# Two cross attentions: every transposed probability block evicted by VectorE, with new written-out orders

## The chip, the cores and the metric

The kernel runs on one core of one Trainium2 chip. The metric is the device time of one execution in microseconds (us), from the start to the end of the program on that core; the median of a few executions is given. Shorter is better. Engines are TensorE (PE in the rows, its weight loads PEld), VectorE (DVE), ScalarE (ACT), GpSimd (POOL) and SyncE (SP, which only issues DMAs here).

## The reference, cut to what matters

A decoder of two layers on x of 16 batches x 256 positions x 512 features, all float32. In order: causal self attention with rotary embedding, causal cross attention, an expert layer, a normalised linear attention, a cross attention without mask, an fp8 linear layer. The change concerns the two cross attentions:

```python
Q = heads(layernorm(x) @ Wq.T + bq); K = heads(ctx @ Wk.T + bk); V = heads(ctx @ Wv.T + bv)   # 16 heads of 32
scores = Q @ K.T / sqrt(32)            # 256 x 256 per head; the first cross attention adds a causal mask
attn = softmax(scores)                 # over the keys
x = x + merge_heads(attn @ V) @ Wo.T + bo   # the first cross attention has no biases
```

## The kernel before, in words

The program is a sequence of phases, one per layer part; each phase is one call that loads its weights, runs over the 16 batches and ends with a barrier over all engines. `attention_phase` builds the self attention ("self") and the two cross attentions ("cross0", causal, and "cross1"). A batch is 256 query positions (two blocks of 128), 16 heads. In a cross attention four heads share one 128-row group g, so there are four groups.

Inside a phase nothing is scheduled at run time. Each engine walks through a written-out order, `ORDERS[phase][engine]`, once per round, a round being one batch in the steady state; a "+" after a step means that it is done for the next batch, a "-" for the batch before. `over_batches` runs a first round that holds only "+" steps, 16 full rounds (the middle ones in a hardware loop) and a last one with only "-" steps. Engines meet only by semaphores. The steps, by their name in the orders:

- X0, X1, C0, C1: TensorE transposes the normalised x or the context into a projection bank (L485); ScalarE writes the high part (L661), VectorE the low part (L735), because projections are made as three products of high and low parts (L73 to L75).
- Q0 to Q3: query and key projection of a group, 24 matmuls; ScalarE evicts Q (L670, L672), VectorE K (L757, L759). V00, V01: values, evicted by VectorE (L750). O0, O1: output projection, added to the residual by VectorE (L768).
- S0 to S3: scores of the four heads of a group into four banks, one per head (L562, with mask L569). A group needs all four banks, so it waits until the exponentials of the group before are done.
- max h (VectorE, L809 or L811), exp h (ScalarE, L678, with the row sums), inv h (VectorE reciprocal, L816), norm h (GpSimd, L431): the softmax of head h.
- T h: TensorE transposes the probabilities of head h into the single bank TP (L590): three 128x128 blocks in cross0, four in cross1. take h: TP is copied to `probT` in SBUF, by ScalarE (L685) or VectorE (L821). T of head h+1 waits for the take of head h (`wait_taken`, in `prob_transposes`).
- PV g: probabilities times values of four heads into the single bank Z (L608); it waits for the takes of its heads and for Z to be free. z g: ScalarE evicts the high part of Z (L692, L694), VectorE the low part (L832, L834).

The projection banks are two and used in turn by the X, C, Q, V and O steps in TensorE's order; class `Uses` counts these uses. A wait for bank use u is a wait on semaphore `a_free` for a count, and since batches run in a loop the count is (batch times uses per batch) plus a constant; `after` makes such a wait. Before the change, ScalarE's order holds the takes of the odd heads and VectorE's those of the even ones in both cross attentions. PV then waits on two semaphores, `pt_act` and `pt_dve`.

Of the kernel before, what the change touches and what calls it, by code (L numbers as in the profile page):

```python
# [30 lines left out]
T = S // P  # L31
# [92 lines left out]
class Uses:  # L124
# [13 lines left out]

    def at(self, key, n):
        i = self.place(key)  # L140
        return (n + (1 - self.keys[i][1])) * self.n + self.before + i
# [5 lines left out]
    def adds(self, key, n):  # L147
# [4 lines left out]
        while True:  # L152
# [3 lines left out]
            if r > self.n_batch or batch_of(r, self.keys[i][1], self.n_batch) is not None:  # L156
# [29 lines left out]
                "Q2 T13- S1 T14- PV2- T15- Q3 T0 PV3- X0+ T1 S2 T2 X1+ V00 T3 V01 T4 S3 T5 O0- C0+ T6 PV0 C1+ T7 O1- T8 Q0+ T9 "  # L186
                "Q1+ T10 S0+ T11 PV1 T12"),
        "ACT": (
                "exp3 Q2 take13- z2- take15- exp4 exp5 exp6 Q3 exp7 X0+ take1 X1+ exp8 exp9 exp10 exp11 take3 z3- take5 exp12 "
                "C0+ exp13 C1+ take7 z0 Q0+ take9 exp14 exp15 Q1+ take11 exp0+ z1 exp1+ exp2+"),  # L190
        "DVE": (
# [3 lines left out]
        "POOL": (  # L195
                "norm10- norm11- norm12- norm13- norm14- norm15- norm0 norm1 rstd+ norm2 norm3 norm4 norm5 norm6 norm7 norm8 "
                "norm9"),
# [3 lines left out]
                "T11- S0 T12- Q2 T13- PV2- T14- Q3 T15- S1 T0 X0+ PV3- T1 V01 T2 V00 T3 S2 C0+ T4 O0- C1+ T5 PV0 X1+ T6 O1- T7 "  # L201
                "S3 T8 Q0+ T9 PV1 T10 Q1+"),
        "ACT": (
                "exp0 exp1 exp2 take13- Q2 z2- exp3 Q3 take15- X0+ z3- take1 exp4 exp5 exp6 exp7 take3 C0+ exp8 exp9 C1+ take5 "
                "exp10 exp11 X1+ z0 take7 exp12 Q0+ take9 exp13 exp14 exp15 Q1+ take11 z1"),
        "DVE": (
# [10 lines left out]
def attention_phase(nc, name, n_batch, x_in, x_out, consts, wq, wk, wv, wo,  # L217
# [42 lines left out]
    with Phase(nc, name) as ph:  # L260
# [195 lines left out]
        def _(pe):  # L456
            pe.wait_ge(const_in, 16 * N_CONST)

            def bank_for(key, n):

                u = uses.at(key, n)
                if not isinstance(u, int) or u > 1:
                    pe.wait_ge(a_free, u - 1)
                return A[uses.bank(key)]
# [1323 lines left out]
```

## Time and profile before

| what | value |
|---|---|
| median of 3 runs | 4003.99 us (4002.36 to 4004.89) |
| the profiled execution | 4007.67 us, its span 4005.9 us |
| mean granted TensorE clock | 0.921 of full speed |
| busy share PE, PEld, DVE, ACT, POOL | 86%, 60%, 49%, 32%, 35% |
| cross0, from its first barrier to its last | about 1251.6 to 1933.6 us of the span |
| cross1, likewise | about 3140.5 to 3853.5 us |
| self attention; experts and linear attention between; fp8 layer | before 1251; 1934 to 3140; after 3854 us |

The span runs from the first to the last instruction; the 1.8 us between it and the execution's own time lie around it. Busy shares are means over all phases. Matmuls overlap one another, so PE busy for 100% of a stretch says that no gap was seen, not that the array is at its peak; whether it waits is read from the idle time before an instruction and from the distance between starts. A duration given for a VectorE or ScalarE instruction includes its start and its end, which overlap with the neighbours, so that back-to-back instructions start closer together than they last.

### The profile page before, as it was taken

The page shows a single profiled execution, that of the slowest core. Times are in us where ns is not written, and L with a number is a line of the kernel's source. Part 1 is how long each engine was busy: PE and PEld are TensorE (multiplying, and loading weights), DVE is VectorE, ACT ScalarE, POOL GpSimd, SP SyncE. Part 2 cuts the span into 40 slices and gives each one's busy share as a digit, 9 for nine tenths or more (in the row PEclk, how much of TensorE's full clock was granted, in tenths as well). Part 3 has the DMA queues.
Part 4 walks back from the last instruction along what each step waited for, and adds up shares of the span by engine and source line. Part 5 has one row for each costly group of instructions (what it writes and reads, how often), then busy time and mean ns, then how long its engine had stood idle before and what let it go on. Part 6 is the DMA issues. An engine that isn't in the chain of part 4 may idle for free. (4 is left out here: it accounts for less than half of the span.)

```text
span 4005.9 us, 71048 instructions
## 1 busy us (share of the span) xinstructions
PE 3444.4 (86%) x23116; PEld 2412.7 (60%) x23116; DVE 1974.0 (49%) x4934; ACT 1263.5 (32%) x4320; POOL 1408.4 (35%) x2092
## 2 busy tenths in 40 slices
PE   4999999999997999999667666655999699999955
PEld 3776776776764888888352111113777578888831
DVE  5555554554553665666420000002666466666667
ACT  2222232232222555555100000001111266666621
POOL 2554554554551443343100000000222155555537
PEclk9999999999997999999857877877999799999976
DMA  5000000000002111110459999994121211111113
GB/s 126 22 16 16 31 16 24 24 16 31 16 11 86 36 60 54 50 63 32 164 173 425 427 427 427 427 427 184 69 70 63 83 37 58 42 63 42 53 66 131
DMA packets 158786, 459.15 MB, mean 115 GB/s; under 512 B 47392, under 2 KB 51872, under 8 KB 138208
## 3 DMA queue, kind: packets, MB, share of 16 engines
q1 hardware_dynamic: 150272, 445.72, 29.3%
q10 hardware_dynamic: 8448, 12.59, 0.9%
q8 instruction: 36, 0.59, 0.1%
q14 instruction: 30, 0.25, 0.0%
HBM read 402.17 MB, written 56.10 MB: 114 GB/s over the span
## 5 line engine op out<-in xcount | busy, mean ns | idle before, releaser
L431 POOL TENSOR_TENSOR cross_prob<-cross_prob,cross_rsum 128x256 f32<-128x256 f32 (+1 forms) x1024 | 547.1, 562 | 725.8 <-DVE cross_rsum L816 721.6
L678 ACT ACTIVATE cross_prob<-cross_S,cross_neg_max 128x256 f32<-128x256 f32 (+1 forms) x1024 | 444.1, 457 | 53.6 <-DVE cross_neg_max L811 46.2
L431 POOL TENSOR_TENSOR self_prob<-self_prob,self_rsum 128x128 f32<-128x128 f32 (+1 forms) x512 | 246.3, 506 | 193.7 <-DVE self_rsum L816 189.4
L590 PE MATMUL cross_T<-cross_ident,cross_prob 128*128 128x128 f32 x1792 | 289.1, 278 | 11.0 <-DVE cross_probT L821 7.7
L1217 PE MATMUL experts_H<-moe_w,experts_tok 128*32 128x512 f32 x1024 | 168.7, 818 | 140.2 <-DMA moe_b<-in_L_ffn_w 135.6
L590 PEld LDWEIGHTS cross_T<-cross_ident,cross_prob 128*128 128x128 f32 x1792 | 205.0, 141 | 70.8 <-issue 38.2
L821 DVE COPY cross_probT<-cross_T 128x384 f32<-128x384 f32 (+1 forms) x256 | 158.6, 620 | 165.5 <-PE cross_T L590 165.5
L678 ACT ACTIVATE self_prob<-self_S,self_neg_max 128x128 f32<-128x128 f32 (+1 forms) x512 | 208.9, 422 | 82.6 <-DVE self_neg_max L809 82.6
L534 PE MATMUL self_A<-self_wo_f,self_zT 128*128 128x512 f32 x512 | 225.1, 593 | 0.6 <-DVE self_zT L828 0.6
L1357 POOL MEMSET norm_minus_half<- 128x2 f32 x1 | 0.1, 104 | 636.3 <-POOLq L53 636.3
L678 ACT ACTIVATION_READ_ACCUMULATOR cross_prob<-cross_S,cross_neg_max 128x1 f32 x1024 | 222.5, 217 | 0.0
L1235 PE MATMUL experts_O<-moe_w,experts_hidT 128*32 128x512 f32 x1024 | 169.0, 821 | 51.2 <-DMA moe_w<-in_L_ffn_w 45.4
L1277 DVE COPY experts_hidT<-experts_T 128x512 f32<-128x512 f32 x32 | 22.1, 691 | 381.1 <-PE experts_T L1228 381.1
L685 ACT ACTIVATE self_probT<-self_T 128x384 f32<-128x384 f32 x128 | 62.9, 491 | 454.3 <-PE self_T L590 454.3
L1217 PEld LDWEIGHTS experts_H<-moe_w,experts_tok 128*32 128x32 f32 x1024 | 44.5, 143 | 263.6 <-issue 257.0
L423 POOL TENSOR_TENSOR self_q_t<-self_q_t,self_turn 128x512 f32<-128x512 f32 x64 | 82.2, 1284 | 320.9 <-DVE self_turn L874 320.7
L811 DVE TENSOR_REDUCE cross_neg_max<-cross_S 128x2 f32<-128x512 f32 x256 | 166.2, 681 | 26.0 <-PE cross_S L562 25.9
L685 ACT ACTIVATE cross_probT<-cross_T 128x384 f32<-128x384 f32 (+1 forms) x256 | 138.7, 542 | 115.8 <-PE cross_T L590 113.7
L534 PEld LDWEIGHTS self_A<-self_wo_f,self_zT 128*128 128x128 f32 x512 | 94.9, 190 | 108.6 <-issue 107.8
L809 DVE TENSOR_REDUCE self_neg_max<-self_S 128x1 f32<-128x128 f32 (+1 forms) x512 | 154.2, 348 | 9.8 <-PE self_S L569 8.9
L73 PE MATMUL cross_A<-cross_xTh,cross_wqh 128*128 128x256 f32 x512 | 156.4, 305 | 3.1 <-DVE cross_xTl L735 1.6
L809 DVE TENSOR_REDUCE cross_neg_max<-cross_S 128x1 f32<-128x128 f32 (+1 forms) x512 | 150.8, 347 | 12.4 <-PE cross_S L569 12.1
(270 smaller groups left out, 8941.6 us busy)
## 6 DMA issues: line engine op xcount, KB each, us to landing
moe_w<-in_L_ffn_w SPq DMA_DIRECT2D x64, 4096.0 KB, 34.8
cross_x_t<-x SPq DMA_DIRECT2D x32, 512.0 KB, 5.1
cross_c_t<-in_ctx SPq DMA_DIRECT2D x32, 512.0 KB, 6.2
cross_res<-x SPq DMA_DIRECT2D x32, 512.0 KB, 3.6
x<-cross_res SPq DMA_DIRECT2D x32, 512.0 KB, 2.8
self_x_t<-in_x SPq DMA_DIRECT2D x16, 512.0 KB, 4.6
self_res<-in_x SPq DMA_DIRECT2D x16, 512.0 KB, 3.5
x<-self_res SPq DMA_DIRECT2D x16, 512.0 KB, 2.8
```

Of the source, the lines that this page charges most:

```text
L73: pe.matmul(out, ah, bh, start=first, stop=False)
L423: pool.tensor_tensor(dst, dst, turns[:, t % 2, :], ALU.add).then_inc(rot, 1)
L431: ins = pool.tensor_tensor(pr, pr, rsum[:, h, t:t + 1].to_broadcast([P, KQ[t]]), ALU.mult)
L534: mm = pe.matmul(out[:, :], zT[:, k, t * P:(t + 1) * P], wo_f[:, k, :], start=(k == 0), stop=(k == NT - 1))
L590: mm = pe.transpose(TP[:, o:o + P], prob[:, h % NP, SOFF[t] + k * P:SOFF[t] + (k + 1) * P], ident[:, :])
L678: ins = act.activation(prob[:, h % NP, SOFF[t]:SOFF[t] + KQ[t]], SC[h % 4][:, SOFF[t]:SOFF[t] + KQ[t]], ACT.Exp, bias=neg_max[:, h, t:t + ...
L685: act.activation(probT[:, h % NPT, :], TP[:, 0:SW], ACT.Copy).then_inc(pt_act, 1)
L809: ins = dve.tensor_reduce(neg_max[:, h, t:t + 1], SC[h % 4][:, SOFF[t]:SOFF[t] + KQ[t]], AX.X, ALU.max, negate=True)
L811: ins = dve.tensor_reduce(neg_max[:, h, :], SC[h % 4][:, :].rearrange("p (t k) -> p t k", t=T), AX.X, ALU.max, negate=True)
L821: dve.tensor_copy(probT[:, h % NPT, :], TP[:, 0:SW]).then_inc(pt_dve, 1)
L1217: pe.matmul(HP[s][32 * n:32 * n + 32, :], tok[:, s, k, :], w1_s[s][:, k, n * 512:(n + 1) * 512], start=(k == 0), stop=False, tile_position ...
L1235: mm = pe.matmul(OP[s][32 * n:32 * n + 32, :], hidT[:, s, q, 32 * n:32 * n + 32], w2_s[s][:, n, q, :], start=(q == 0), stop=(q == NQ - 1), ...
```

## The change

In cross0 and cross1 the takes of the odd heads leave ScalarE's order and enter VectorE's, so that VectorE takes all 16 heads and ScalarE none. All four orders of both phases are written anew. On TensorE the set of steps is the same, in another order. The self attention keeps its orders. Besides, waits of TensorE on `a_free` that stood behind one another are made into one wait for the larger count: at the first users of the new x and context, and before PV, where the two waits for V become one. These last edits also reach the self attention. With all takes on one engine `times_v` waits on one semaphore for them instead of two.

```diff
@@ -136,9 +136,13 @@
     def place(self, key):
         return [k for k, _ in self.keys].index(key)
 
+    def count(self, key):
+
+        i = self.place(key)
+        return (1 - self.keys[i][1]) * self.n + self.before + i
+
     def at(self, key, n):
-        i = self.place(key)
-        return (n + (1 - self.keys[i][1])) * self.n + self.before + i
+        return n * self.n + self.count(key)
 
     def bank(self, key):
         assert self.n % 2 == 0
@@ -183,33 +187,35 @@
     },
     "cross0": {
         "PE": (
-                "Q2 T13- S1 T14- PV2- T15- Q3 T0 PV3- X0+ T1 S2 T2 X1+ V00 T3 V01 T4 S3 T5 O0- C0+ T6 PV0 C1+ T7 O1- T8 Q0+ T9 "
-                "Q1+ T10 S0+ T11 PV1 T12"),
+                "Q2 T13- S1 T14- PV2- T15- Q3 T0 PV3- V01 T1 S2 T2 V00 T3 O0- T4 C0+ PV0 T5 C1+ X0+ T6 S3 X1+ T7 O1- T8 Q0+ T9 "
+                "PV1 T10 S0+ T11 Q1+ T12"),
         "ACT": (
-                "exp3 Q2 take13- z2- take15- exp4 exp5 exp6 Q3 exp7 X0+ take1 X1+ exp8 exp9 exp10 exp11 take3 z3- take5 exp12 "
-                "C0+ exp13 C1+ take7 z0 Q0+ take9 exp14 exp15 Q1+ take11 exp0+ z1 exp1+ exp2+"),
+                "exp3 Q2 z1- z2- exp4 Q3 exp5 exp6 exp7 z3- exp8 exp9 exp10 C0+ exp11 C1+ X0+ X1+ exp12 exp13 z0 exp14 Q0+ "
+                "exp15 exp0+ exp1+ Q1+ exp2+"),
         "DVE": (
-                "stats+ Q2 inv2 take14- max4 max5 max6 max7 z2- apply+ take0 Q3 X0+ inv3 max8 inv4 max9 take2 inv5 inv6 max10 "
-                "X1+ max11 z3- V00 take4 V01 max12 inv7 inv8 max13 O0- take6 C0+ inv9 inv10 C1+ max14 inv11 inv12 take8 O1- "
-                "inv13 z0 Q0+ max15 take10 inv14 max0+ max1+ Q1+ max2+ inv15 take12 inv0+ max3+ inv1+ z1"),
+                "max5 inv1 inv2 z2- take15- Q2 inv3 max6 max7 take0 Q3 inv4 stats+ inv5 inv6 z3- take1 V01 max8 take2 max9 inv7 "
+                "apply+ V00 take3 max10 max11 inv8 inv9 take4 O0- C0+ take5 C1+ take6 X0+ max12 take7 X1+ max13 inv10 inv11 "
+                "max14 inv12 max15 inv13 take8 z0 O1- take9 Q0+ take10 take11 max0+ max1+ inv14 max2+ take12 inv15 max3+ inv0+ "
+                "Q1+ take13 z1 take14 max4+"),
         "POOL": (
-                "norm10- norm11- norm12- norm13- norm14- norm15- norm0 norm1 rstd+ norm2 norm3 norm4 norm5 norm6 norm7 norm8 "
-                "norm9"),
+                "norm11- norm12- norm13- norm14- norm15- norm0 norm1 norm2 norm3 norm4 norm5 norm6 rstd+ norm7 norm8 norm9 "
+                "norm10"),
     },
     "cross1": {
         "PE": (
-                "T11- S0 T12- Q2 T13- PV2- T14- Q3 T15- S1 T0 X0+ PV3- T1 V01 T2 V00 T3 S2 C0+ T4 O0- C1+ T5 PV0 X1+ T6 O1- T7 "
-                "S3 T8 Q0+ T9 PV1 T10 Q1+"),
+                "T11- S0 T12- Q2 T13- PV2- T14- S1 T15- Q3 T0 PV3- T1 V01 T2 S2 T3 V00 T4 O0- C0+ T5 PV0 C1+ T6 X0+ S3 T7 X1+ "
+                "O1- T8 Q0+ T9 PV1 T10 Q1+"),
         "ACT": (
-                "exp0 exp1 exp2 take13- Q2 z2- exp3 Q3 take15- X0+ z3- take1 exp4 exp5 exp6 exp7 take3 C0+ exp8 exp9 C1+ take5 "
-                "exp10 exp11 X1+ z0 take7 exp12 Q0+ take9 exp13 exp14 exp15 Q1+ take11 z1"),
+                "exp4 Q2 exp5 z3- exp6 Q3 exp7 exp8 exp9 exp10 C0+ exp11 C1+ X0+ X1+ exp12 exp13 z0 z1 Q0+ exp14 exp15 Q1+ "
+                "exp0+ exp1+ exp2+ exp3+ z2"),
         "DVE": (
-                "z1- take12- max3 inv0 stats+ take14- inv1 Q2 apply+ z2- inv2 take0 Q3 max4 X0+ inv3 max5 max6 inv4 V01 inv5 "
-                "max7 take2 inv6 z3- inv7 V00 max8 max9 C0+ take4 max10 inv8 O0- inv9 max11 C1+ take6 X1+ inv10 inv11 z0 max12 "
-                "take8 max13 max14 max15 O1- take10 inv12 inv13 Q0+ Q1+ inv14 max0+ max1+ max2+ inv15"),
+                "max7 Q2 take0 inv3 inv4 stats+ inv5 inv6 take1 inv7 Q3 take2 V01 max8 z3- take3 max9 apply+ max10 V00 take4 "
+                "inv8 max11 O0- take5 C0+ inv9 take6 C1+ X0+ inv10 take7 X1+ max12 max13 max14 take8 z0 O1- inv11 take9 inv12 "
+                "max15 Q0+ inv13 take10 z1 take11 Q1+ max0+ take12 max1+ max2+ max3+ inv14 inv15 inv0+ take13 take14 inv1+ "
+                "max4+ inv2+ max5+ z2 take15 max6+"),
         "POOL": (
-                "norm13- norm14- norm15- res- norm0 rstd+ norm1 norm2 norm3 norm4 norm5 norm6 norm7 norm8 norm9 norm10 norm11 "
-                "norm12"),
+                "norm0 norm1 res- norm2 norm3 norm4 norm5 norm6 rstd+ norm7 norm8 norm9 norm10 norm11 norm12 norm13 norm14 "
+                "norm15"),
     },
 }
 
@@ -456,11 +462,13 @@
         def _(pe):
             pe.wait_ge(const_in, 16 * N_CONST)
 
-            def bank_for(key, n):
-
-                u = uses.at(key, n)
-                if not isinstance(u, int) or u > 1:
-                    pe.wait_ge(a_free, u - 1)
+            def taken(n, keys, before=()):
+
+                after(pe, a_free, n, uses.n, max([uses.count(k) + 1 for k in keys] + [uses.count(k) - 1 for k in before]))
+
+            def bank_for(key, n, keys=()):
+
+                taken(n, keys, [key])
                 return A[uses.bank(key)]
 
             def full(mm, key, n):
@@ -487,11 +495,8 @@
 
             def project(key, n, part):
 
-                out = bank_for(key, n) if part != 1 else A[uses.bank(key)]
-                if key == X_USER and part != 1:
-                    pe.wait_ge(a_free, uses.at(("X", 1), n) + 1)
-                if key == C_USER and part != 1:
-                    pe.wait_ge(a_free, uses.at(("C", 1), n) + 1)
+                new = [("X", 1)] * (key == X_USER) + [("C", 1)] * (key == C_USER)
+                out = bank_for(key, n, new) if part != 1 else A[uses.bank(key)]
                 if key[0] == "P":
                     mm = proj_tokens(out, xT, (wqs, wks)[key[1]], key[3], key[2], part)
                 else:
@@ -510,12 +515,12 @@
 
             def q_and_k(key, n, part):
                 g = key[1]
-                out = bank_for(key, n) if part != 1 else A[uses.bank(key)]
+                out = bank_for(key, n, [("X", 1)] * (key == X_USER)) if part != 1 else A[uses.bank(key)]
                 for j, (w, src) in enumerate(((wqs, xT), (wks, cT))):
                     if part is not None and part != j:
                         continue
-                    if key == (X_USER, C_USER)[j]:
-                        pe.wait_ge(a_free, uses.at(("XC"[j], 1), n) + 1)
+                    if j == 1 and key == C_USER:
+                        taken(n, [("C", 1)])
                     mm = split_products(pe, out[:, j * S:(j + 1) * S], [
                         ((w[0][:, k, g * P:(g + 1) * P], w[1][:, k, g * P:(g + 1) * P]),
                          (src[0][:, k, :], src[1][:, k, :])) for k in range(KD)])
@@ -599,8 +604,7 @@
                         wait_taken(n, mine[-1], off)
                 c = g * G * d_head // 512
                 if g == 0 or (g - 1) * G * d_head // 512 != c:
-                    for t in range(T):
-                        pe.wait_ge(a_free, uses.at(("V", c, t), n) + 1)
+                    taken(n, [("V", c, t) for t in range(T)])
                 after(pe, z_ok, n, NT, g, off)
                 for k in range(T):
                     for hh in heads:
```

## Rows read from the trace of the kernel before

**Rows 1.** Windows, rounds of cross0, cross1: us, PE PEld DVE ACT POOL busy, clock, DMA

```profile
1336.36:1375.44 39.08, 39.08 (x371) 32.59 (x370) 24.58 (x81) 21.59 (x85) 15.85 (x33) 1.00 0.16 55
3296.50:3337.28 40.78, 40.78 (x354) 33.43 (x353) 28.23 (x64) 25.16 (x84) 22.09 (x36) 1.00 0.16 51
```

**Rows 2.** Waits of PE, cross0 at 1320:1880, then cross1 at 3200:3800 (us, times, longest)

```profile
PE cross_T L590 <- POOL cross_prob L431: 0.8, 1, 0.8
...
PE cross_T L590 <- DVE cross_probT L821: 1.3, 2, 0.9
```

**Rows 3.** Tile cross_T: PE's idle time before it, whole program (us, times)

```profile
  POOL cross_prob L431: 13.1, 24
  DVE cross_probT L821: 10.7, 25
  ACT cross_probT L685: 7.1, 18
```

**Rows 4.** Groups by line and shape, cross1 at 3200:3800 (busy us, mean ns)

```profile
L821 DVE COPY cross_probT<-cross_T 128x512 f32<-128x512 f32 x119 | 81.6, 686 | 57.1 <-PE cross_T L590 57.1
L685 ACT ACTIVATE cross_probT<-cross_T 128x512 f32<-128x512 f32 x118 | 70.2, 595 | 24.5 <-PE cross_T L590 23.9
L759 DVE TENSOR_SCALAR cross_KT<-cross_A,cross_bk_c 128x256 f32<-128x256 f32 x59 | 27.8, 471 | 33.5 <-ACT cross_QT L672 33.5
```

**Rows 5.** The same view, cross0 at 1320:1880

```profile
L821 DVE COPY cross_probT<-cross_T 128x384 f32<-128x384 f32 x115 | 63.6, 553 | 83.8 <-PE cross_T L590 83.8
```

**Rows 6.** Timeline of PE in a steady round of cross1 (start us, us)

```profile
3271.09 0.60 PE L590 MATMUL cross_T<-cross_ident,cross_prob 128*128 128x128 f32 x4
3271.62 1.07 PE L608 MATMUL cross_Z<-cross_probT,cross_V 128*32 128x256 f32 x16
3272.62 0.66 PE L590 MATMUL cross_T<-cross_ident,cross_prob 128*128 128x128 f32 x4
...
3275.96 0.60 PE L590 MATMUL cross_T<-cross_ident,cross_prob 128*128 128x128 f32 x4
3276.49 1.15 PE L562 MATMUL cross_S<-cross_KT,cross_QT 32*128 32x256 f32 x16
3277.57 0.66 PE L590 MATMUL cross_T<-cross_ident,cross_prob 128*128 128x128 f32 x4
```

**Rows 7.** Timeline of PE in the last batch of cross1

```profile
3825.60 1.15 PE L562 MATMUL cross_S<-cross_KT,cross_QT 32*128 32x256 f32 x16
...
3829.77 0.66 PE L590 MATMUL cross_T<-cross_ident,cross_prob 128*128 128x128 f32 x4
3831.30 0.63 PE L590 MATMUL cross_T<-cross_ident,cross_prob 128*128 128x128 f32 x4 [0.88 <-DVE cross_probT L821]
3832.83 0.63 PE L590 MATMUL cross_T<-cross_ident,cross_prob 128*128 128x128 f32 x4 [0.90 <-ACT cross_probT L685]
```

**Rows 8.** Timeline of DVE in the same stretch

```profile
3826.76 0.69 DVE L811 TENSOR_REDUCE cross_neg_max<-cross_S 128x2 f32<-128x512 f32 x1 [0.44 <-PE cross_S L562]
3827.37 0.69 DVE L821 COPY cross_probT<-cross_T 128x512 f32<-128x512 f32 x1
3827.98 1.88 DVE L811 TENSOR_REDUCE cross_neg_max<-cross_S 128x2 f32<-128x512 f32 x3
...
3830.46 0.69 DVE L821 COPY cross_probT<-cross_T 128x512 f32<-128x512 f32 x1
3831.07 0.42 DVE L816 RECIPROCAL cross_rsum<-cross_sums 128x2 f32<-128x2 f32 x3
```

**Rows 9.** Timeline of PE in the last batch of cross0

```profile
1907.32 0.52 PE L590 MATMUL cross_T<-cross_ident,cross_prob 128*128 128x128 f32 x3 [0.67 <-ACT cross_probT L685]
1908.58 0.60 PE L590 MATMUL cross_T<-cross_ident,cross_prob 128*128 128x128 f32 x3 [0.74 <-DVE cross_probT L821]
```

**Rows 10.** Timeline of ACT in cross1, two heads' exponentials apart

```profile
3811.03 0.49 ACT L678 ACTIVATE cross_prob<-cross_S,cross_neg_max 128x256 f32<-128x256 f32 x1
...
3811.93 0.50 ACT L678 ACTIVATE cross_prob<-cross_S,cross_neg_max 128x256 f32<-128x256 f32 x1
```

## The prediction

> **What bounds the kernel now.** I read the page first: PE is busy 86% of the span against 49% for DVE (table above). That is a mean over phases, so the second view is the busy time by window, for one round of each cross attention [rows 1]. A round of cross0 lasts 39.08 us, one of cross1 40.78 us, PE is busy in all of it at the full clock, DVE for 24.58 and 28.23 us, ACT for 21.59 and 25.16 us. Third, the waits of PE [rows 2]: in 560 us of cross0 it waits 0.8 us for the data of a T step, in 600 us of cross1 1.3 us. So the steady rounds are as long as TensorE's own work. The idle time in front of T over the whole program is 30.9 us (13.1 + 10.7 + 7.1) [rows 3]; nearly all of it must therefore lie in the first and last batches of the phases, where there is too little other work between two T steps. Neither ScalarE nor VectorE is the bound, and a lighter ScalarE gives nothing by itself. The change can only gain by shortening PE's own sequence or those ends, and it loses wherever VectorE is late.
>
> **What is removed and added.** Per batch, eight takes leave ACT, 8 x 0.595 = 4.8 us in cross1 [rows 4], and go to DVE at 0.686 us in cross1 and 0.553 us in cross0 [rows 4, 5]: 5.5 and 4.4 us. DVE's busy time in a round becomes 28.2 + 5.5 = 33.7 of 40.8 us (83%) and 24.6 + 4.4 = 29.0 of 39.1 us (74%). It still fits, so the average is no bound; what counts is whether DVE is free at the moments when PE needs it. What hides the takes is the PE step between two Ts.
>
> **PE's own work.** Each round has the same 36 steps. What follows a T starts 0.53 us after it whether it is PV with its two take semaphores, or S, whose waits stay as they are (3271.09 to 3271.62, 3275.96 to 3276.49 [rows 6]). So the waits that the change merges or drops cost PE nothing that shows, there and in the self attention; I take 0. The new neighbours (T before C, C before X, X before O) are not all in the trace; with two or three changed joints per round and some 0.05 us each, either way, over 30 rounds: 0, with bounds of -3 and +3 us.
>
> **The short pairs.** A take is hidden if T, the steps between and the next T take longer than the chain T, take, T. The chain alone can be seen in the last batch: 3829.77 to 3831.30 = 1.53 us over VectorE, 3831.30 to 3832.83 = 1.53 us over ScalarE [rows 7]; the take starts 0.69 us after T (3830.46 [rows 8]), and the next T 0.84 us after that. In the steady round T, PV, T takes 1.53 us and T, S, T 0.53 + 1.08 = 1.61 us [rows 6]. So in cross1 a PV between two Ts covers the chain with nothing to spare, an S with 0.08. The new order of cross1 has six such pairs per round (S between T11 and T12, T14 and T15, T2 and T3; PV between T13 and T14, T0 and T1, T9 and T10), the old one five; in three of the new (T11, T13, T9) the take moves from ScalarE to VectorE. In cross0 the chain over VectorE is 1.26 us (1907.32 to 1908.58), with 0.74 us idle against 0.67 over ScalarE [rows 9]; there one pair with only a PV (T9, T10) changes engine, at 0.07 us.
>
> Does the engine matter here? By these rows a take by VectorE delays the next T by 0 in cross1 and 0.07 us in cross0: 0.07 x 15 = 1 us. The Trainium skill ("VectorE: DVE Perf Modes", Specifications) speaks against the change: VectorE sits closer to SBUF and ScalarE closer to PSUM; its table of cycles for PSUM to SBUF (the section on the TRN2 errata) gives 658 ns and 570 ns for 512 elements, an estimate of 0.09 us more per take. At the three pairs with a PV where the engine changes that would be 3 x 0.09 x 15 = 4 us. The durations agree with the page (686 and 595 ns), the distance between Ts in cross1 doesn't, so the sum goes by the rows.
>
> **The tightest place in cross1.** The new order puts S1 between T14 and T15, then Q3, T0, PV3, T1. From the start of S1, PE needs 1.08 to T15, 3.34 (T and Q, 3272.62 to 3275.96) to T0 and 1.53 to T1 [rows 6]: T1 at 5.95. On VectorE max4 can start 1.16 after S1 (3825.60 [rows 7], 3826.76 [rows 8]). Behind it in the new order stand max5, max6, max7, z2, take15, the K eviction Q2, two inverses, and take0. Starts lie 0.60 us apart for a max and 0.61 for a take (3827.98 with three in 1.88; 3827.37 to 3827.98 [rows 8]); the 256-wide instructions last 0.471 [rows 4], less the overlap of 0.08 that the others have, 0.39; an inverse takes 0.07 to 0.14 (three in 0.42 [rows 8]). Sum: 1.16 + 4 x 0.60 + 0.61 + 2 x 0.39 + 0.14 to 0.28 = 5.09 to 5.23. take0 could start at 4.42 + 0.69 = 5.11. VectorE is on time or 0.12 us late; I take 0.06, 0.9 us over 15 rounds. S1 itself comes one projection earlier than before and needs exp3 of the next batch: from S0 PE needs 1.08 + 3.34 + 1.53 + 0.53 = 6.5 us. The first max starts at 1.16, the first exp some 0.7 later, and four heads of exp take 4 x 0.90 [rows 10] = 3.6, with 0.3 lost to take12 between the maxima: 5.8. That fits, by 0.7 us. In the pair T2, S2, T3, VectorE's K eviction of Q3 stands ahead of take2 and waits for ScalarE, which waits for PV3 (its z3) and two heads of exp: 0.2 + 0.4 + 0.9 + 0.4 = 1.9 us after PV3 ends, then the inverse of exp7, 0.9 + 0.15, and the eviction 0.4: 3.4. T2 starts some 3.3 us after T1 (a V is about as long as a Q), and take2 may start 0.69 later, 4.0. Covered by 0.5. GpSimd's res step moves behind norm0 and norm1; norm2 is then the first that could be late; T2 comes 9 us after S1, at which norm1 can start, and GpSimd is busy 22 of 40.8 us [rows 1], so I take 0. No DMA moves.
>
> **The tightest place in cross0.** T4, C0, PV0, T5, C1, X0, T6: VectorE has take4, the eviction of O0, the low part of C0 and take5 in a row, 0.47 + 0.60 + 0.60. With take4 starting 0.56 after T4, take5 starts at 2.2 us and lets T6 start 0.70 later, at 2.9; PE would be there at 2.85. Late by 0.07 us: 1 us over 15 rounds. (0.56 and 0.70 split the 1.26 of [rows 9].)
>
> **Ends of the phases.** Both orders have the same number of Ts in the last batch with nothing between them, and the chain costs 0 or 0.07 us more [rows 7, 9]. In the first batch V01 now hides take0 in cross0 but O0 (empty there) no longer hides take3: a gap of one chain less a T moves. I take +0.5; bounds -4 and +4, from the 30.9 us of [rows 3], shared by six ends.
>
> **Sum.** Pairs +1.0, cross1 +0.9, cross0 +1.0, ends +0.5, the rest 0: +3.4 us, to be set against the profiled execution: 4005.9 + 3.4 us of span and 1.8 around it, 4011.1. That execution lies 3.7 us over the median of the runs shown (4003.99), so for the median I predict 4007.4 us. A measurement of this kernel can tell some 0.2% (8 us) from no change; this is inside.
>
> **Rivals.**
> - Slower: VectorE in queue order holds a take back. The take is one of 16 in a strict order, between maxima of 0.6 us. If my walk misses half a max (0.3 us) at three of the six short pairs of cross1, that is 0.3 x 3 x 15 = 13 us, 4017 to 4021; it decides from 0.27 us per round, averaged over both phases (8 us in 30 rounds). For it: VectorE at 83%, and spare times of 0 to 0.12 us. Against it: the old order had pairs of 1.53 us as well and PE's waits are 1.3 us in all [rows 2]; work waits ahead of a take only in the places walked above. Chance 0.26.
> - Faster: the gaps after T are not pipeline filling but waits that the sequencer takes one after another. Then the merged waits (one per PV, three more at X, C and V, 7 per round) give back a part of the 0.53 us between a T and what follows, from 0 to 0.2 each; at 0.1, 7 x 0.1 x 30 = 21 us, 3983 to 3986. Against it: the gap after T is 0.53 before S as well [rows 6]. Chance 0.08, for this and any gain at the ends.
> - No change in substance: what I forecast, TensorE sets the round and all takes stay hidden. Chance 0.66.
>
> **The numbers.** The middle case spans 3999 to 4012 with the bounds above (joints 3 us, ends 4 us, not both at full size). Adding most of the slower rival's cases and little of the faster one gives 3998 to 4021. Faster 0.08, within 0.2% 0.66, slower 0.26.
>
> **What would show it.** Right: rounds of 39.1 to 39.3 and 40.7 to 40.9 us, PE busy in all of them, DVE at about 29 and 33.7 us, idle time of PE before T that names only DVE and stays under 5 us in the steady stretches. The step on cross1's tightest place is right if the idle time there sits before T1. Wrong: a round of cross1 above 41 us with PE waiting for DVE cross_probT (the slower rival), waits for ACT cross_prob at S1 (exp3 late), or T, PV, T in less than 1.53 us (the faster one).

## The result, and the profile after

Timed side by side, the changed kernel takes 4011.0 us (20 runs, 4007.2 to 4016.8) and the kernel before 4004.6 us (20 runs, 3998.2 to 4012.4): ratio 1.0016, interval 1.0009 to 1.0023, 6.4 us slower. The forecast was 3.4 us more. The profiled execution of the changed kernel took 4013.1 us, its span 4011.3 us.

The same views as in [rows 1], [rows 2] and [rows 3]. First the windows of one round (us, then busy time of PE, PEld, DVE, ACT and POOL, the clock, the DMA share), O0 to O0:

```profile
1336.00:1375.13 39.13, 39.13 (x370) 32.57 (x370) 28.31 (x90) 18.68 (x76) 16.26 (x34) 1.00 0.16 55
3291.80:3332.63 40.83, 40.83 (x354) 33.31 (x353) 32.85 (x72) 21.08 (x76) 21.80 (x36) 1.00 0.15 51
```

TensorE is busy all of the time in both, as before; a round became 0.05 us longer in cross0 and 0.05 here in cross1; over the 13 steady intervals from O0 to O0 the mean rose by 0.06 (39.13, 39.07) and 0.08 (40.83, 40.75). VectorE went up by 3.7 and 4.6 us, ScalarE down by 2.9 and 4.1. The waits of PE: none at 1320:1880, and at 3200:3800 (us, times, longest):

```profile
PE cross_T L595 <- DVE cross_probT L825: 1.3, 2, 0.9
PE cross_A L493 <- DVE cross_V L754: 0.5, 1, 0.5
PE cross_A L73 <- DVE cross_xTl L739: 0.4, 1, 0.4
```

The tile cross_T, idle time of PE before it in the whole program; ScalarE is gone from it, the sum is 32.3 us against 30.9:

```profile
  POOL cross_prob L437: 20.3, 48
  DVE cross_probT L825: 12.0, 15
```

The groups by shape, cross1 and then cross0 (busy us, mean ns), answer to [rows 4] and [rows 5]: twice the takes at the same price.

```profile
L825 DVE COPY cross_probT<-cross_T 128x512 f32<-128x512 f32 x236 | 162.1, 687 | 82.5 <-PE cross_T L595 79.4
L825 DVE COPY cross_probT<-cross_T 128x384 f32<-128x384 f32 x230 | 127.9, 556 | 142.0 <-PE cross_T L595 139.6
```

So the steady rounds account for little: 13 x 0.06 + 13 x 0.08 = 1.8 us (1.9 from the unrounded means). The waits view lists none of it: a step late by 0.03 or 0.1 us shows only in the distance between starts. What it can't list is read from the starts of the steps. The timeline of PE around the place that the prediction called the tightest of cross1 (start us, us), matmuls of the projections left out:

```profile
3274.42 1.15 PE L567 MATMUL cross_S<-cross_KT,cross_QT 32*128 32x256 f32 x16
3275.50 0.66 PE L595 MATMUL cross_T<-cross_ident,cross_prob 128*128 128x128 f32 x4
...
3278.85 0.60 PE L595 MATMUL cross_T<-cross_ident,cross_prob 128*128 128x128 f32 x4
3279.38 1.07 PE L612 MATMUL cross_Z<-cross_probT,cross_V 128*32 128x256 f32 x16
3280.41 0.63 PE L595 MATMUL cross_T<-cross_ident,cross_prob 128*128 128x128 f32 x4
...
3283.72 0.63 PE L595 MATMUL cross_T<-cross_ident,cross_prob 128*128 128x128 f32 x4
```

These are S1, T15, T0, PV3, T1 and T2. T0 to T1 takes 1.56 us, 0.03 more than a T, a PV and nothing else. T1 to T2 with the value projection V01 between takes 3.31 us. What VectorE does meanwhile:

```profile
3279.57 0.69 DVE L825 COPY cross_probT<-cross_T 128x512 f32<-128x512 f32 x1
3280.18 0.22 DVE L820 RECIPROCAL cross_rsum<-cross_sums 128x2 f32<-128x2 f32 x2
3280.31 1.27 DVE L723 BATCH_NORM_STATS2 cross_stats<-cross_x_t 128x6 f32<-128x512 f32 x2
...
3281.90 0.96 DVE L729 TENSOR_SCALAR cross_rstd<-cross_mv 128x2 f32<-128x2 f32 x1
3282.77 0.21 DVE L820 RECIPROCAL cross_rsum<-cross_sums 128x2 f32<-128x2 f32 x2
3282.91 0.66 DVE L825 COPY cross_probT<-cross_T 128x512 f32<-128x512 f32 x1
```

take0 starts at 3279.57; take1, for which T2 waits, only at 3282.91, 2.50 us after T1 began. Ahead of it stand the layer norm statistics of the next batch, and among them one instruction on 128x2 elements that takes 0.96 us.

### The profile page after: what moved, and what is told of

The parts are those of the page before. It is cut to its first block and busy times, and to the rows that moved or that the text cites. A ratio compares the mean times of both kernels' runs of the same rounds, so it can differ in the third digit from the quotient of the medians.

```text
span 4011.3 us, 70885 instructions
## 1 busy us (share of the span) xinstructions
PE 3441.9 (86%) x23108; PEld 2410.9 (60%) x23116; DVE 2106.8 (53%) x5190; ACT 1150.8 (29%) x4064; POOL 1410.0 (35%) x2092
## 5 line engine op out<-in xcount | busy, mean ns | idle before, releaser
L825 DVE COPY cross_probT<-cross_T 128x384 f32<-128x384 f32 (+1 forms) x512 | 318.2, 621 | 242.2 <-PE cross_T L595 236.4
L682 ACT ACTIVATION_READ_ACCUMULATOR cross_prob<-cross_S,cross_neg_max 128x1 f32 x1024 | 210.6, 206 | 0.0
L75 PE MATMUL cross_A<-cross_xTh,cross_wql 128*128 128x256 f32 x512 | 145.9, 285 | 0.0
```

The costliest lines, as they stand in the source:

```text
L75: mm = pe.matmul(out, al, bh, start=False, stop=last)
L682: ins = act.activation(prob[:, h % NP, SOFF[t]:SOFF[t] + KQ[t]], SC[h % 4][:, SOFF[t]:SOFF[t] + KQ[t]], ACT.Exp, bias=neg_max[:, h, t:t + ...
L825: dve.tensor_copy(probT[:, h % NPT, :], TP[:, 0:SW]).then_inc(pt_dve, 1)
```

## The experiments

**Theory A**: the loss is in the attentions, some 0.05 and 0.08 us per round through late takes, and the rest at the ends of the phases. **Theory B**: it is not in these orders at all; phases without a change differ by as much. Between one barrier over all engines and the next, the untouched phases indeed scatter: the stretch between the two cross attentions took 1206.7, 1204.1 and 1209.9 us in three profiles with the old orders, 1209.1, 1206.2 and 1208.1 in three with the new. But everything outside the two cross attentions together took 2612.8 us in the mean with the old orders and 2611.8 with the new, 1 us less: theory B fails. (Each ratio below is estimated from all runs of the two kernels and isn't the quotient of the two medians; where the two differ, the ratio with its interval is the better number.)

**new_again**: the changed kernel once more, no edit.

> The changed kernel itself, once more, for comparison with its own parts on one chip. Theory A (the steady rounds cost 0.05 us more in cross0 and 0.08 us in cross1, 2 us in all, and the ends of the phases the rest, partly through TensorE's clock): 3 to 8 us above the kernel before, rounds of 39.12 and 40.83 us again; the last output projection of cross1 may or may not run at the low clock again. Theory B (the difference is made outside the cross attentions, by code that isn't changed): the barrier-to-barrier times of cross0 and cross1 together stay within 1 us of before and the other phases are longer.

4011.5 us beside 4006.0, ratio 1.0015 (1.0006 to 1.0024). The difference is real, and it is 0.15%.

**merged_waits_only**: the changed code with the four orders of before.

```diff
-                "T11- S0 T12- Q2 T13- PV2- T14- S1 T15- Q3 T0 PV3- T1 V01 T2 S2 T3 V00 T4 O0- C0+ T5 PV0 C1+ T6 X0+ S3 T7 X1+ "
-                "O1- T8 Q0+ T9 PV1 T10 Q1+"),
+                "T11- S0 T12- Q2 T13- PV2- T14- Q3 T15- S1 T0 X0+ PV3- T1 V01 T2 V00 T3 S2 C0+ T4 O0- C1+ T5 PV0 X1+ T6 O1- T7 "
+                "S3 T8 Q0+ T9 PV1 T10 Q1+"),
...
```

This is TensorE in cross1; the other engines and cross0 go back in the same way.

> The orders of before, the merged waits of after. If TensorE's separate waits cost nothing that shows (my prediction), same as before within 2 us in every phase, rounds 39.07 and 40.75 us. If the merged waits save time (my faster rival), faster by 5 to 20 us, and then the new orders cost that much more than the total shows. The self attention, shorter by 1.3 us in the profile of after, shows it alone.

4004.8 us, ratio 0.9999 (0.9991 to 1.0008), rounds 39.06 and 40.75 as before. The merged waits cost and give nothing that shows, neither here nor in the self attention, which ends at 1253.1 us of the span against 1251.3 and 1253.3 in two profiles of the old code. The second take semaphore is still waited for in this run, since half of the takes are ScalarE's; that dropping it gives nothing is read from the distance from T to PV in cross1, 0.53 us in both kernels. The mirror image, the old code with the new orders, wasn't tried.

**new_cross0_only** and **new_cross1_only**: the new orders in one phase alone.

> New orders in cross0, old ones in cross1. Theory A: cross0 rounds 39.12 us, cross0 within 1 us of before, total 0 to +2 us. Theory B: as far above before as the full change.

> New orders in cross1, old ones in cross0. Theory A: cross1 rounds 40.83 us, cross1 2 to 3.5 us longer than before in the profile, total +2 to +5 us. Theory B: as the full change, with cross1 itself no longer than before.

4006.6 us, 1.0006 (0.9997 to 1.0014), and 4009.5 us, 1.0004 (0.9995 to 1.0012). Each round keeps its value: 39.14 and 40.75 in the first, 39.06 and 40.83 in the second. The rounds of one phase don't depend on the orders of the other; how the loss divides between them the times alone can't say, since neither interval excludes 1.

**stats_late**: in cross1, take1 goes ahead of the statistics on VectorE.

```diff
-                "max7 Q2 take0 inv3 inv4 stats+ inv5 inv6 take1 inv7 Q3 take2 V01 max8 z3- take3 max9 apply+ max10 V00 take4 "
+                "max7 Q2 take0 inv3 inv4 take1 stats+ inv5 inv6 inv7 Q3 take2 V01 max8 z3- take3 max9 apply+ max10 V00 take4 "
```

> The changed kernel with one step moved: in VectorE's order of cross1, take1 stands ahead of stats instead of behind stats, inv5 and inv6. Theory A: of the 0.08 us that a round of cross1 lost, the wait of T2 for take1 is the largest part (V01 to T2 took 2.92 instead of 2.83 to 2.86 us), because take1 is held back by stats with a 128x2 instruction that took 0.95 us there; rounds of 40.74 to 40.77 us. Rival: VectorE is late for its load as a whole, the wait only moves to T3; rounds stay at 40.83 us. Total within 3 us of the changed kernel either way.

4008.4 us beside 4006.9, ratio 1.0009 (1.0000 to 1.0018). The round of cross1 is 40.70 us, 0.13 less than with the change, 0.05 less than before it and less than the 40.74 to 40.77 expected. What the run does to the total is within the intervals. The windows view and, in PE's timeline, T1 and T2:

```profile
3289.44:3330.14 40.70, 40.70 (x354) 33.39 (x353) 32.26 (x72) 21.11 (x76) 21.82 (x36) 1.00 0.16 52
```

```profile
3278.16 0.63 PE L595 MATMUL cross_T<-cross_ident,cross_prob 128*128 128x128 f32 x4
...
3281.37 0.60 PE L595 MATMUL cross_T<-cross_ident,cross_prob 128*128 128x128 f32 x4
```

T1 to T2 is 3.21 us instead of 3.31 (and T2 to S2 0.53 instead of 0.56): what stood ahead of take1 was the late work. VectorE's groups by shape at 3210:3795 (count, busy us, mean ns) show what the small instruction costs in the kernel before, in the changed one and here, one fence for each:

```profile
L725 DVE TENSOR_SCALAR cross_rstd<-cross_mv 128x2 f32<-128x2 f32 x14 | 7.6, 543 | 0.5
```
```profile
L729 DVE TENSOR_SCALAR cross_rstd<-cross_mv 128x2 f32<-128x2 f32 x14 | 12.8, 913 | 0.5
```
```profile
L729 DVE TENSOR_SCALAR cross_rstd<-cross_mv 128x2 f32<-128x2 f32 x14 | 2.4, 170 | 0.5
```

What differs is what GpSimd does meanwhile. Its timeline in the changed kernel, and then in stats_late:

```profile
3279.35 3.49 POOL L437 TENSOR_TENSOR cross_prob<-cross_prob,cross_rsum 128x256 f32<-128x256 f32 x6
3283.01 2.32 POOL L437 TENSOR_TENSOR cross_prob<-cross_prob,cross_rsum 128x256 f32<-128x256 f32 x4 [0.17 <-DVE cross_rsum L820]
```
```profile
3277.11 3.48 POOL L437 TENSOR_TENSOR cross_prob<-cross_prob,cross_rsum 128x256 f32<-128x256 f32 x6
3281.45 2.33 POOL L437 TENSOR_TENSOR cross_prob<-cross_prob,cross_rsum 128x256 f32<-128x256 f32 x4 [0.87 <-DVE cross_rsum L820]
```

In the changed kernel the instruction of VectorE (3281.90 to 3282.86) ends when, to 0.02 us, GpSimd's six normalisations end (3279.35 + 3.49 = 3282.84). In stats_late it starts at 3281.11, between two bursts of GpSimd (3280.59 to 3281.45), and takes 0.17 us. In the three traces of the changed kernel it takes 0.17 us in all 51 places where no GpSimd instruction lies beside it, and 0.29 to 0.96 us in the 45 where one does, ending each time within 0.03 us of the end of one.

That its length, and not the statistics as such, makes take1 late is to be seen where it happens to be short with the order unchanged. In the third batch of the changed kernel it took 0.36 us, take1 started 1.90 us after T1 and T2 came 3.24 us after it; in the rounds with 0.96 us these distances are 2.50 and 3.31 us. In late_take (below) it took 0.30 us in every steady round, and T2 came 3.22 us after T1 although an added copy stood ahead of take1 too. So about 0.07 of the 0.10 us are this one instruction's.

The rule that fits is in the Trainium skill ("SBUF — State Buffer", Who interferes with whom): one pair of SBUF ports is shared by the two engines as an exclusive lock, taken for a whole instruction. It names tensor_scalar among the operations that can use both pairs, but no length; here, by the 0.96 us beside 0.17, it would have caught an instruction of 128x2 elements. The trace agrees with a lock, but shows only the times, not the ports. The instruction overlapped two of GpSimd's and ended with the second, so it did not get through between them.

**takes_back**: the odd heads' takes go back to ScalarE (in cross1 all but head 13's), TensorE's orders stay the new ones. I placed the takes in ScalarE's orders by hand; they go out of VectorE's. ScalarE's order in cross0:

```diff
-                "exp3 Q2 z1- z2- exp4 Q3 exp5 exp6 exp7 z3- exp8 exp9 exp10 C0+ exp11 C1+ X0+ X1+ exp12 exp13 z0 exp14 Q0+ "
-                "exp15 exp0+ exp1+ Q1+ exp2+"),
+                "exp3 Q2 take13- z1- z2- take15- exp4 Q3 exp5 exp6 exp7 z3- take1 exp8 exp9 take3 exp10 C0+ exp11 take5 C1+ X0+ X1+ "
+                "take7 exp12 exp13 z0 exp14 Q0+ take9 exp15 exp0+ exp1+ take11 Q1+ exp2+"),
```

> The changed kernel's TensorE and GpSimd orders, but the odd heads' takes back on ScalarE (in cross1 without take13). Theory A (the cost is the queue in which the take stands, not TensorE's new order): rounds of cross0 at 39.05 to 39.10 and of cross1 at 40.75 to 40.80 us; T9, PV1, T10 in cross0 0.02 to 0.05 us shorter. Rival (TensorE's new order with its new neighbours costs the time): rounds stay 39.12 to 39.15 and 40.83 us. Second rival (ScalarE close to PSUM matters more than the rows of before say): rounds below 39.05 and 40.75 us.

4009.7 us, ratio 1.0006 (0.9997 to 1.0015); rounds of 39.31 and 40.72 us. In cross1 the 0.1 us is gone (40.75 to 40.80 us was expected): the small instruction takes 0.96 us there as well, but take1 no longer stands behind it. In cross0 the place X0, T6 is on time, as PE's timelines show, of the changed kernel and of this one:

```profile
1349.04 0.49 PE L595 MATMUL cross_T<-cross_ident,cross_prob 128*128 128x128 f32 x3
...
1351.51 0.62 PE L493 MATMUL cross_A<-cross_ident,cross_x_t 128*128 128x128 f32 x4
1352.06 0.52 PE L595 MATMUL cross_T<-cross_ident,cross_prob 128*128 128x128 f32 x3
```
```profile
1350.57 0.49 PE L587 MATMUL cross_T<-cross_ident,cross_prob 128*128 128x128 f32 x3
...
1353.03 0.62 PE L485 MATMUL cross_A<-cross_ident,cross_x_t 128*128 128x128 f32 x4
1353.48 0.49 PE L587 MATMUL cross_T<-cross_ident,cross_prob 128*128 128x128 f32 x3
...
1363.97 0.94 PE L559 MATMUL cross_S<-cross_KT,cross_QT 32*128 32x128 f32 x16 [0.24 <-ACT cross_prob L674]
```

T4 to T6 takes 3.02 us with VectorE's takes and 2.91 without. That this round is longer all the same (39.31 where 39.05 to 39.10 was expected) comes from my order: a take ahead of exp15 makes S0 wait for ScalarE in each of 15 rounds, with 0.24 us of idle time, and T10 to S0 takes 0.79 us instead of 0.45. Less these 0.34 us the round would be 38.97 us, an estimate: 0.1 below the old one. So in cross0 TensorE's new order by itself seems to be shorter, and the takes on VectorE to cost more than that; no run has these orders without the wait at S0.

**late_take**: VectorE copies 128 columns more, into a spare tile, ahead of each take of both cross attentions.

```diff
+                if not rotary:
+                    dve.tensor_copy(spare[:, h % 8, :], TP[:, 0:128])
```

> The changed kernel with an extra copy of 128 columns of the transposed block, some 0.2 us, in front of every take of both cross attentions (its result is not used). It prices the slower rival. If the short pairs are the only tight places, each that has no spare time lengthens by 0.2 us: in cross1 three pairs with a PV by 0.2 and three with an S by 0.12, 0.96 us per round; in cross0 three pairs (T14 to T15, T9 to T10, T5 to T6), 0.6 us per round; rounds of 39.7 and 41.8 us, the total 20 to 28 us over the changed kernel. If VectorE's load makes it late in further places: over 42.5 us in cross1, 35 us or more in all. If there was hidden slack after all: under 10 us.

4035.9 us (4 runs), ratio 1.0071 (1.0055 to 1.0086): some 22 us over the changed kernel by the two ratios, inside the 20 to 28 expected. Rounds 39.87 and 41.36 us; 39.7 and 41.8 were expected. By the starts of the steps the delay appears behind the short pairs, in cross1 with less than the 0.2 us of the copy: S and PV between two Ts grow from 1.08 and 1.00 to between 1.14 and 1.24 us. In cross0 two PVs grow from 0.81 to 1.01, and in the place with C1 and X0 between T5 and T6 these grow from 0.44 and 0.56 to 0.59 and 0.75. The long steps cover it. The waits of PE (cross0, then cross1) name the take, though only part of the time:

```profile
PE cross_T L597 <- DVE cross_probT L829: 4.1, 27, 0.2
...
PE cross_T L597 <- DVE cross_probT L829: 4.2, 17, 1.1
```

So VectorE's lateness does cost time on this path, as the slower rival had it, once it is there. The change made too little of it.

**warm_new** and **warm_old**: idle work for TensorE in the last batch, behind T12 to T15, on stats_late and on merged_waits_only.

```diff
+                        if not rotary and isinstance(r, int) and n == n_batch - 1 and key[1] > 11:
+                            for i in range(5):
+                                pe.transpose(SC[key[1] % 4][:, 0:P], ident[:, :], ident[:, :])
```

> The orders of stats_late, and in the last batch of each cross attention five transposes of the identity (0.7 us of TensorE work, into a bank of scores that nobody reads any more) behind each of T12 to T15, where TensorE has 0.9 us of idle time before the next T. Theory A (a part of the loss lies in the last batch: TensorE idles, its granted clock falls to the lower level, and the last outputs run slower): the clock stays at 1.00 to the end of cross1, the last O0 there takes 3.2 us instead of 5.3, from its start to the barrier 10.8 us instead of 12.9 to 13.9; the time is 2 to 5 us below stats_late (4008.4 beside 4006.9 of before), so 4003 to 4006 beside 4006. Theory B (the loss is in rounds or in other phases, the clock at the end is only a companion): the same time as stats_late within 1 us, or 1 to 2 us more for the added work.

> The same idle work with the orders of before (and the changed code of the waits). In the three profiles with these orders the clock at the end of cross1 was high anyway, so theory A expects cross1 unchanged (within 1 us) and a gain of 0 to 3 us at most, from the end of cross0: 4001 to 4005 beside 4005. Theory B: no difference, within 1 us. Should warm_new and warm_old come out alike, the orders themselves are worth nothing once the ends are equal.

4006.1 and 4005.4 us beside 4003.6: ratios 1.0004 (0.9995 to 1.0013) and 0.9997 (0.9988 to 1.0006). The times can't resolve it, and of traces there is one for each. Windows of 6 us each before the end of cross1 (us, busy times, then the clock, last but two), stats_late and then warm_new:

```profile
3831.90:3837.90 6.00, 3.47 (x41) 2.08 (x44) 3.29 (x7) 0.47 (x1) 4.78 (x6) 0.99 0.20 76
3837.90:3843.90 6.00, 4.83 (x21) 3.17 (x14) 0.48 (x1) 0.47 (x1) 0.00 (x0) 0.50 0.00 0
3843.90:3849.90 6.00, 4.26 (x16) 2.80 (x15) 1.32 (x2) 0.00 (x0) 0.00 (x0) 0.94 0.00 0
```
```profile
3829.10:3835.10 6.00, 3.99 (x39) 2.85 (x40) 3.26 (x7) 1.74 (x8) 4.31 (x8) 1.00 0.42 140
3835.10:3841.10 6.00, 4.25 (x38) 3.00 (x39) 2.25 (x4) 0.95 (x2) 2.60 (x3) 1.00 0.01 3
3841.10:3847.10 6.00, 5.03 (x22) 3.61 (x20) 0.69 (x1) 0.00 (x0) 0.00 (x0) 1.00 0.00 0
```

And PE's timeline: T15, the first matmul of the last O0 and the last one of O1, again stats_late first:

```profile
3835.91 0.63 PE L595 MATMUL cross_T<-cross_ident,cross_prob 128*128 128x128 f32 x4 [0.88 <-DVE cross_probT L825]
...
3840.03 0.80 PE L73 MATMUL cross_A<-cross_woh,cross_zTh 128*128 128x512 f32 x1 [1.17 <-DVE cross_zTl L838]
...
3848.75 0.39 PE L75 MATMUL cross_A<-cross_woh,cross_zTl 128*128 128x512 f32 x1
```
```profile
3836.54 0.63 PE L595 MATMUL cross_T<-cross_ident,cross_prob 128*128 128x128 f32 x4 [0.33 <-DVE cross_probT L828]
...
3840.21 0.50 PE L73 MATMUL cross_A<-cross_woh,cross_zTh 128*128 128x512 f32 x1 [1.19 <-DVE cross_zTl L841]
...
3846.85 0.39 PE L75 MATMUL cross_A<-cross_woh,cross_zTl 128*128 128x512 f32 x1
```

From the start of T15 to that of the last matmul of O1 it is 12.8 us where the granted clock fell to 0.50 (the 1.2 GHz level) and 10.3 us where it stayed at 1.00 (2.4 GHz): 2.5 us for one end of one phase. From the last O0's start to cross0's barrier the two profiles differ in the same way, 12.9 and 10.8 us. That the idle work is what held the clock up isn't shown: without it the clock was high under these outputs in three of seven profiles of the new order (below), and in cross0 of warm_new it fell all the same, to 0.73 in the mean of 1908.4 to 1914.4, ahead of the outputs.

**third_new** and **old_copy**: the two kernels of the comparison once more, on the same chip.

> The changed kernel once more, for a third profile and a third comparison: 1.0015 by both theories. Theory A: the last O0 of cross1 takes over 5 us at a granted clock below 0.9 again. Theory B: it takes 3.2 us here, and the time is the same.

> The kernel before, as a measure of the comparison itself: ratio 1.0000 within 0.0009. Its profile: theory A expects the clock at the end of cross1 at 1.00 and the last O0 there at 3.2 us, as in the three profiles with the old order of cross1; theory B has no expectation for it. The phases without a change are expected to differ from the first profile by up to 2 us each.

Ratios 1.0022 (1.0013 to 1.0031) and 0.9996 (0.9987 to 1.0005). This time the clock at the end of cross1 was high with the new orders too, the last O0 took 3.2 us up to its eviction, and the kernel was slower all the same (4014.1 us beside 4003.6; old_copy 4002.5). So theory A's expectation about the clock failed: the change doesn't force it down there. With TensorE's new order of cross1 it was low under the last outputs in the changed kernel's first two profiles, in stats_late and in late_take, and high in third_new, new_cross1_only and takes_back; with the old order the last outputs ran at the high clock in every profile (before, merged_waits_only, new_cross0_only, old_copy). In cross0 it was low in three of four profiles with the old orders (all but old_copy) and in six of seven with the new ones (all but new_again). The windows over the last part of cross1, of before and of after:

```profile
3832.00:3838.00 6.00, 4.24 (x28) 2.23 (x28) 1.28 (x4) 2.12 (x6) 5.00 (x8) 0.72 0.39 136
...
3844.00:3850.00 6.00, 4.38 (x19) 3.02 (x17) 1.19 (x2) 0.00 (x0) 0.00 (x0) 1.00 0.00 0
```
```profile
3838.00:3844.00 6.00, 3.16 (x33) 1.34 (x25) 2.38 (x5) 0.95 (x2) 3.54 (x4) 0.81 0.00 0
3844.00:3850.00 6.00, 5.12 (x12) 3.71 (x12) 0.69 (x1) 0.00 (x0) 0.00 (x0) 0.62 0.00 0
```

In both the clock falls once in the drain, where PE is busy for 3 to 4 us of 6. Before, it fell under T13 (1.09 us long at 3834.33) and PV2 and was back at 1.00 for the outputs; after, it fell under PV3 (1.51 us long at 3841.27) and the output projection. The order alone doesn't decide it: with the same orders as before merged_waits_only and old_copy had no fall in cross1's drain at all, and new_cross1_only had none with the new one.

**Where the time is.** From barrier to barrier, us, three profiles of each of the two kernels (before, old_copy and, as the third with the old orders, merged_waits_only; after, new_again, third_new):

| phase | old orders | new orders | difference of the means |
|---|---|---|---|
| cross0 | 681.8, 676.4, 680.5 | 681.4, 677.8, 681.6 | +0.7 |
| cross1 | 712.8, 709.5, 710.0 | 715.7, 718.7, 713.7 | +5.2 |

Together +5.9 us, beside 6.4, 6.0 and 8.8 us from the three ratios (0.0016, 0.0015 and 0.0022 of 4004). Of cross1's 5.2 the first 13 intervals between the O0 steps hold 13 x 0.08 = 1.0, the last one 0.8 (40.72 against 39.89 us: the steps for a next batch fall away there, and in the new order they left a hole that nothing filled), and of the rest 3.2 lie in the drain of the last batch and 0.1 in the fill; in two of the three profiles the outputs at the low clock have over 2 us of it (from the last O0 to the barrier 13.0 and 13.2 us against 10.8 in the others). Cross0 fills faster by 3.5 us (its first O0 comes 96.2 us after the barrier against 99.7) and gives that back in its last full round (39.1 against 38.0 us) and the drain.

Most of cross1's drain is the clock. Where it never fell after the fill (new_cross1_only against merged_waits_only and old_copy), the time from the first O0 to the barrier is 606.2 us against 604.0: the 1.0 and 0.8 of the rounds and only 0.3 in the drain. In cross0 the clock never fell after the fill in new_again and old_copy; there the whole phase is 1.4 us longer, with 4.0 gained in the fill, 1.0 and 1.1 lost in the rounds and 3.3 in the drain. So at the full clock the change would cost some 3.6 us, an estimate from these few profiles, and the rest is where the clock fell.

## Why the prediction was right, and where it was off

- **Side and size.** 4007.4 us against 4011.0: slower, within 0.2%, inside the range. Of the difference, 0.6 us is that the kernel before measured 4004.6 and not 4004.0 in this comparison; the remaining 3.0 is the sum of the change, +3.4 forecast and +6.4 measured. In the three pairs of profiles the terms for the rounds, forecast +2.9, come to +1.9 and the ends, forecast +0.5, to +4.0.
- **The bound.** TensorE sets the round, all of 39.13 and 40.83 us. Right; VectorE at 28.3 and 32.9 us was forecast at 29.0 and 33.7, the difference being the overlap of 0.08 us that successive instructions have and the sum of durations counts twice.
- **Merged waits at nothing.** Right (0.9999). The faster rival falls with it.
- **PE's own joints, 0 with 3 either way.** Inside the bounds, but not 0: once take1 is on time the new order of cross1 is 0.05 us per round shorter than the old, although T1 is still 0.03 late, and in cross0 the late places make 0.13 us where the round grew by 0.066. That is some 0.08 and 0.06 us per round, about -1.9 us in 13 rounds of each.
- **Short pairs.** In cross1 the engine made no difference, as the 1.53 us of [rows 7] said: T13 to T14 over VectorE with only a PV between took 1.53 (1.56 where a queue stood ahead). In cross0 T9 to T10 takes 0.81 us from PV1 to T10 against 0.79 over ScalarE, 0.02 where I had 0.07. The 4 us that the Trainium skill's table would give ("VectorE: DVE Perf Modes", the section on the TRN2 errata) aren't there: its difference of 0.09 us per take is in the durations (687 and 595 ns) and not in the distance from T to T.
- **Tightest place of cross1.** The walk along VectorE's queue put take0 5.11 us after S1's start; it came at 5.15 (3279.57 less 3274.42). T1 was late by 0.03 us, 0.06 forecast. S1 in its early place never waited for exp3. All right.
- **What the walk left out.** It followed K evictions, maxima and takes, and took up the queue again only at K's eviction ahead of take2. The pair T1, V01, T2 looked safe with 3.2 us between, so the step "stats+" ahead of take1 was not priced. It cost 0.13 us per round, 1.7 us in 13 rounds, mostly by one instruction of 0.96 us whose length depends on what GpSimd does meanwhile. The row with 543 ns for that instruction was to be had in the trace before. That the sum of the rounds came near all the same is luck: this cost and the gain in the joints, both taken as nothing, cancel.
- **15 rounds.** The prediction multiplied by 15; an O0 follows an O0 in a steady round 13 times, and the last full round, where the steps for a next batch fall away, is a case of its own (+0.8 us in cross1, +1.1 in cross0). The spare time ahead of take2, given as 0.5 us, is 0.6 by its own numbers (4.0 less 3.4); nothing hung on it.
- **Tightest place of cross0.** 0.07 us late forecast, 0.11 measured (3.02 less 2.91).
- **The ends, +0.5 with 4 either way.** This is the term that was mis-sized: +4.0 measured, at the upper bound, with 3.2 us in cross1's drain, 0.8 in its last full round, 0.1 in its fill and -0.1 in cross0 as a whole. At the full clock it would be some 1.6. I counted the chains and didn't follow what happens to the holes of the missing "+" steps, nor the clock. [Rows 7] contained a sign of it: Ts in a row with 0.9 us of idle time ahead of each.
- **The slower rival.** It decided from 0.27 us per round; VectorE held takes back by 0.02 to 0.11 us at four places (T1 and T2 of cross1, T6 and T10 of cross0). late_take shows that the mechanism works as described.

What stays open: whether the new order of cross1 makes a fall of the clock under the output projection likelier, or whether 4 of 7 against 0 of 4 profiles is chance; and how much of the three ratios' 6 to 9 us is in cross0, where the profiles of one kernel differ by 5 us. No version was found that beats the kernel before: with the new orders the best, warm_new, is at 1.0004, and with the old ones warm_old's 0.9997 can't be told from 1.

## What to carry over

Walk every queue through the whole round and not only through its tight places: the one costly instruction was a tiny one, ahead of a take that had 3 us to spare. Where one engine sets the round, moving work between the others gives nothing by itself and costs where a step of theirs then comes late; here two thirds of the difference were made in the first and last batch, which the rounds don't show. Differences of a few us in a program with long drains need several profiles of each kernel, because where the clock falls differs from run to run.

## What the runs showed of the hardware

- A TENSOR_SCALAR on 128x2 elements of VectorE takes 0.170 us with GpSimd idle and up to 0.96 us when it meets a run of TENSOR_TENSOR instructions on GpSimd; in 15 batches of cross1 in a row it ended within 0.03 us of the end of one of them (after). Copies from PSUM in the same stretches kept their 0.69 us.
- A 512-element take is 92 ns longer on VectorE than on ScalarE (687, 595), and the distance from T to T is 1.53 us over either.
- With five transposes of an identity, 0.7 us, in each idle gap of 0.9 us TensorE's granted clock was at 1.00 through the last 18 us of cross1 (one profile), where in the profile without them it was at 0.50 for 6.8 us; the work after T15 took 10.3 us instead of 12.8. In the drain of cross0 it fell for 3.4 us in spite of them, and other profiles kept 1.00 without them.
